# Batches 0 to 10 sorted and worked as a set of their own, in groups of four tiles

## The chip, the core and the metric

The kernel runs on one core of a Trainium2 chip. The metric is the device time of one execution in microseconds (us); lower is better. The engines are TensorE (PE; its weight loads are listed apart as PEld), VectorE (DVE), ScalarE (ACT) and GpSimd (POOL); SP issues DMAs only. The engines run side by side, each through its own list of instructions in order, and wait for one another by semaphores.

## The reference

16 batches of 128 rows of width 128 go through two layers. Layer 0 is attention with 16 heads (queries from x, keys and values from 77 context rows and x) and a feed-forward of butterfly matrices; layer 1 is attention over 77 context rows in which each head keeps its 32 largest scores, and then a feed-forward with 8 experts. Cut to the last part, which the change is about:

```python
x = hidden_states.reshape(-1, h)                    # 16 x 128 rows
route = jax.nn.sigmoid(x @ Wr + br)
max_prob = jnp.max(route, axis=1, keepdims=True)
max_ind = jnp.argmax(route, axis=1)
for e in range(n_experts):                          # 8
    mask = (max_ind == e)[:, None].astype(x.dtype)
    y = jax.nn.gelu(x @ W1[e], approximate=False) @ W2[e]
    out = out + mask * y
out = out * max_prob
```

Each row needs one expert only. W1 is 8 x 128 x 512, W2 is 8 x 512 x 128, all float32.

## The kernel before

**The pipeline of batches.** Everything up to the router's logits is done batch by batch in a pipeline of steps (`run_steps`, `step`). In step i six batches are in work: P = i (inputs), A = i-1 and A2 = i-2 (first attention and its output), B = i-3 (feed-forward 0 and the second attention's scores), C = i-4 (its top 32, on DVE with MAX8 and MATCH_REPLACE8), E = i-5 (output, router). Each step has 8 slots, and the code of each engine lists by hand what it does in which slot; a pair such as (17, 5) below is step 17, slot 5. Steps 16 to 20 have no new batch: A is last present in 16, A2 in 17, B in 18, C in 19, E in 20.

**The sorting.** The experts are worked on sorted rows. For a range of batches (`ROUTES`: 0 to 10, 11 to 14, 15) DVE adds the router's bias (`route_biases`), ACT takes the exponential (`route_exps`), DVE finds each row's expert (`choose`), TensorE counts the rows of each expert by matmuls with ones (`count_rows`), and DVE turns the counts into a place for each row (`row_places`). POOL then scatters each batch's 128 rows to DRAM (`place_row`, one indirect DMA each, line 617). With all 16 batches counted, DVE works out for each of 23 tiles of 128 sorted rows which expert it has and where it begins (`map_tiles`). 23 = 16 + 8 - 1 is the most that 2,048 rows in 8 experts can fill.

**The tiles.** Behind the last batch SP loads the tiles (`load_tile`, line 386, into a ring of 12) and ACT's queue loads their W1 (`load_up`). TensorE turns a tile (line 716), multiplies it by W1 (`tile_up`, line 1161), ACT takes the GELU, TensorE multiplies by W2 (`tile_down`, line 1171), DVE scales and adds the residual (line 1771), and POOL scatters the rows to the output (line 704). Two tiles overlap.

The order of everything is the order in which the code is written, engine by engine; there is no scheduler.

## Time and profile before

| | us |
|---|---|
| median of three runs | 732.41 (731.75 to 734.16) |
| the profiled execution | 734.37 |
| its span in the trace | 732.6 |
| busy in it: PE, DVE, ACT, POOL | 651.1, 571.1, 481.2, 446.9 |

The page divides the span into 40 slices of 18.3 us. TensorE is over 90% busy in slices 5 to 31, until about 577 us, and then at 60 to 70%; its granted clock falls there from full speed to half. DVE stays near 90% until about 640 us. From 680 us TensorE is full again, with the 23 tiles. Of the chain that ended last 49% is TensorE and 35% DVE. Times such as "at 577.09" are us from the start of the span.

### The profile page before, as it was taken

What the parts mean: (1) busy time and instruction counts of PE and PEld (TensorE: products, weight loads), DVE (VectorE), ACT (ScalarE), POOL (GpSimd) and SP (SyncE); (2) the same over time, 40 slices, a digit from 0 to 9 for tenths busy, and PEclk for the clock granted to TensorE, in tenths of its full rate; (3) what the DMA queues carried; (4) which work ended last, traced back from release to release, by engine and by line L of the source; (5) the groups of instructions that cost most, each with busy time, mean ns of one, the idle gap of its engine ahead of it and who ended that gap; (6) DMA issues with size and microseconds to landing.
All of it is one profiled execution on the core that took longest, in us unless ns stands there. A gap on an engine that the chain in (4) does not pass through costs nothing.

```text
span 732.6 us, 19295 instructions
## 1 busy us (share of the span) xinstructions
PE 651.1 (89%) x4994; PEld 529.2 (72%) x4994; DVE 571.1 (78%) x3740; ACT 481.2 (66%) x1331; POOL 446.9 (61%) x689
## 2 busy tenths in 40 slices
PE   5588999999999999999999999999999876772995
PEld 4455677778787787878787878778786764551995
DVE  3255747898989999998989898999999998943231
ACT  1247578888878797888878887878787634221221
POOL 7364667857657575756576765757575536543344
PEclk9779999999999999999999999999999755555998
DMA  7300039992000000000000000000000000003772
GB/s 204 76 1 1 1 105 309 318 294 70 1 3 1 1 1 0 0 0 0 0 0 0 0 0 0 0 0 0 0 1 2 1 0 28 32 23 116 210 205 64
DMA packets 38537, 37.92 MB, mean 52 GB/s; under 512 B 3633, under 2 KB 34249, under 8 KB 38484
## 3 DMA queue, kind: packets, MB, share of 16 engines
q1 hardware_dynamic: 32986, 27.76, 13.6%
q10 hardware_dynamic: 3994, 6.36, 3.1%
q0 software_dynamic: 1504, 3.17, 1.2%
q8 instruction: 24, 0.39, 0.2%
q14 instruction: 29, 0.24, 0.1%
HBM read 16.28 MB, written 21.45 MB: 52 GB/s over the span
## 4 chain that ended last, share of the span: by engine, by line
PE 49%; DVE 35%; issue 6%; POOL 3%; SPq 3%; DMA 2%; ACT 2%; DVEq 0%; POOLq 0%
DVE sw L1564 14%; DVE m L1558 9%; PE bank L716 8%; PE bank L874 6%; PE bank L816 5%; PE bank L945 5%; PE bank L884 4%; PE score_banks L846 3%; DVE negmax L1511 3%; PE bank L1161 3%; PE bank L1171 3%; PE bank L826 2%; PE bank L804 2%; PE bank L908 2%; PE bank L899 2%
## 5 line engine op out<-in xcount | busy, mean ns | idle before, releaser
L1564 DVE MATCH_REPLACE8 sw<-m,sw 128x77 f32<-128x77 f32 x1024 | 219.6, 221 | 0.1
L1558 DVE MAX8 m<-sw 128x8 f32<-128x77 f32 x1024 | 188.8, 225 | 2.3 <-ACT sw L1189 1.3
L1189 ACT ACTIVATE prob<-score_banks,negmax 128x205 f32<-128x205 f32 x256 | 107.2, 431 | 21.3 <-DVE negmax L1511 21.3
L485 POOL TENSOR_TENSOR prob<-prob,inv 128x820 f32<-128x820 f32 x64 | 99.4, 1553 | 18.7 <-DVE inv L1516 18.7
L504 POOL TENSOR_TENSOR sw<-sw,m 128x616 f32<-128x616 f32 x64 | 77.9, 1217 | 50.1 <-DVEq L1545 49.7
L945 PEld LDWEIGHTS bank<-v,p1T 77*128 77x128 f32 x512 | 72.6, 216 | 16.3 <-DVE c_z L1590 6.1
L945 PE MATMUL bank<-v,p1T 77*128 (+1 forms) x512 | 72.5, 269 | 10.9 <-DVE c_z L1590 5.4
L1564 DVE MATCH_VALUE_LOAD sw<-m,sw 128x8 f32 x1024 | 76.6, 75 | 0.0
L1511 DVE TENSOR_REDUCE negmax<-score_banks 128x2 f32<-128x410 f32 x128 | 68.1, 573 | 2.7 <-PE score_banks L846 2.7
L716 PE MATMUL bank<-ident,prob 128*77 128x128 f32 (+1 forms) x512 | 67.3, 275 | 1.6 <-POOL prob L485 1.4
L1189 ACT ACTIVATE h_ring<-bank 128x256 f32<-128x256 f32 (+1 forms) x87 | 38.5, 443 | 45.5 <-PE bank L1161 35.5
L826 PE MATMUL bank<-raw,kvT 128*77 128x512 f32 (+1 forms) x128 | 66.7, 603 | 0.0
L716 PEld LDWEIGHTS bank<-ident,prob 128*77 128x77 f32 (+1 forms) x512 | 58.7, 146 | 9.3 <-POOL prob L485 5.1
L816 PE MATMUL bank<-kvT,raw 128*128 128x205 f32 x256 | 60.4, 359 | 1.2 <-DVE xs L1523 0.6
L928 PE MATMUL bank<-second_keys,b_q 128*128 128x308 f32 x128 | 53.2, 500 | 9.1 <-ACT p1T L1189 8.8
L846 PE MATMUL score_banks<-k_sb,q_sb 64*128 64x205 f32 x512 | 58.7, 348 | 0.0
L511 POOL TENSOR_TENSOR p<-sw 128x308 f32<-128x308 f32 x64 | 46.9, 733 | 18.4 <-ACT sw L1189 18.2
L874 PE MATMUL bank<-ptc,z_ring 77*64 77x128 f32 x512 | 53.7, 287 | 3.3 <-issue 2.6
L816 PEld LDWEIGHTS bank<-kvT,raw 128*128 128x128 f32 x256 | 43.2, 192 | 16.1 <-issue 14.5
L1189 ACT ACT_TABLE_LOAD x34 | 43.6, 1283 | 15.9 <-issue 15.3
L1189 ACT ACTIVATION_READ_ACCUMULATOR prob<-score_banks,negmax 128x1 f32 x256 | 52.9, 207 | 0.0
L874 PE MATMUL bank<-ptl,z_ring 128*64 128x128 f32 x512 | 50.6, 274 | 0.0
(235 smaller groups left out, 1446.7 us busy)
## 6 DMA issues: line engine op xcount, KB each, us to landing
z_sorted<-no_row SPq DMA_DIRECT2D x1, 17415.0 KB, 65.6
raw<-in_L_ffn_W ACTq DMA_DIRECT2D x23, 256.0 KB, 3.4
z_ring<-z_sorted SPq DMA_DIRECT2D x23, 129.0 KB, 3.4
w<-in_L_ffn_W SPq DMA_DIRECT2D x8, 256.0 KB, 4.5
raw<-in_L_xattn_Wkv SPq DMA_DIRECT2D x2, 512.0 KB, 11.2
xs<-in_x SPq DMA_DIRECT2D x1, 960.0 KB, 7.2
cx<-in_ctx SPq DMA_DIRECT2D x1, 577.5 KB
raw<-in_L_xattn_Wq SPq DMA_DIRECT2D x1, 512.0 KB, 10.4
```

The lines of the kernel that those rows point to most:

```text
L485: g.tensor_tensor(p, p, inv[:, 4 * q:4 * q + 4].unsqueeze(2).to_broadcast([128, 4, KV]), ALU.mult).then_inc(s["p_norm"], 1)
L504: g.tensor_tensor(v, v, m8[:, 4 * q:4 * q + 4, 0, 0:1].to_broadcast([128, 4, 2 * NK]), ALU.subtract).then_inc(s["sub_done"], 1)
L716: return nc.tensor.transpose(dst, src, ident[0:rows, 0:rows])
L816: last = mm(dst[:, KV * c:KV * c + KV], wkv_in[:, at:at + 128], kvT[:, :], start=True, stop=True)
L826: mm(dst[0:nr, :], kvT[:, r0:r0 + nr], wkv_in[:, INNER + 512 * j:INNER + 512 * j + 512], start=True, stop=True)\
L846: last = mm(SC[:, u, KV * r:KV * r + KV], q_sb[rows[u], q // 2, 2 * (q % 2) + r, :], k_sb[rows[u], q % 2, r, :], start=False, stop=(r == 1 ...
L874: last = mm(dst[64 * u:64 * u + 64, 128 * c:128 * c + 128], v[:, DH * h:DH * h + DH], p[:, 2 * c + u, :], start=not last_part, stop=last_p ...
L945: last = mm(M[:, c:c + D1 + 1], p1T[:, n, :], v1[:, bass.ds(b, 1), 4 * q + n, :].squeeze(1), start=True, stop=True)
L1189: return nc.scalar.activation(dst, src, f, **kw)
L1511: v.tensor_reduce(negmax[:, 2 * p:2 * p + 2], SC[:, :, KV * (p % 2):KV * (p % 2) + KV], AX_X, ALU.max, negate=True).then_inc(s["max_ready" ...
L1558: v.max(m8[:, h, r, :], sw[:, h, src, :]).then_inc(s[name], 1)
L1564: v.match_replace(sw[:, h, 1, :], m8[:, h, r, :], sw[:, h, src, :], TAKEN)\
```

## The change

The rows of batches 0 to 10 become a set of their own, with its own sorted DRAM tensor, counts and map; batches 11 to 15 are the second set. A set of n batches can fill n + 7 tiles: 18 and 12, together 30 in place of 23.

- The choosing for batches 0 to 10 moves from step 17 to step 16 on DVE and ACT, the counting from (17, 5) to (16, 4) on TensorE, into bank M in place of a score bank (DVE copies the counts out first), the places from (17, 7) to (16, 4), and a first `map_tiles` stands at (16, 5) on DVE.
- POOL's eleven scatters, one in each slot of steps 18 and 19 (11 slots) before, stand in four bunches: 3 at (16, 5), 2 at (16, 6), 3 at (17, 2), 3 at (17, 3).
- The 18 tiles are worked in groups of four: TensorE turns four, then four times W1, then four times W2; ACT copies the turned tiles out, takes four GELUs and scales four results; POOL adds the residual for the group and scatters four times. SP loads tiles and W1 of this set.
- Groups 0 and 1 lie in steps 17 to 20. Groups 2, 3 and 4 (4, 4 and 2 tiles) stand behind step 20, with the counting of batch 15 between the second and third tile of group 2. The 12 tiles of the second set follow in the old manner, two by two. SP loads the first four W1 of the second set, and then its tiles.
- W1's ring becomes 4, the rings of turned tiles and GELUs become 4. Some loads at the start share a semaphore. Nothing changes in steps 0 to 15.

```diff
-    SORTED = NB + NE - 1
-    UPS = 3
+    EARLY = 11
+    SETS = ((0, EARLY), (EARLY, NB))
+    TILES = (EARLY + NE - 1, NB - EARLY + NE - 1)
+    FIRST = (0, TILES[0])
+    GROUP = 4
+    GROUPS = (TILES[0] + GROUP - 1) // GROUP
+    SORTED = sum(TILES)
+    UPS = GROUP
     ROW = 2 * D + 2
     COEF, TOKEN = 2 * D, 2 * D + 1
     NOWHERE = 1 << 20
-    ROUTES = ((0, 11), (11, 15), (15, NB))
+    ROUTES = ((0, EARLY), (EARLY, 15), (15, NB))
...
-        PLACE_AT = {(18 + b // 8, b % 8): (b,) for b in range(ROUTES[0][1])}
+        PLACE_AT = {(16, 5): range(0, 3), (16, 6): range(3, 5), (17, 2): range(5, 8), (17, 3): range(8, EARLY)}
+        DRAIN_GROUPS = 2
+        COUNTS_KEPT = 7
...
             sp.wait_ge(s["map_ready"], 2)
-            sp.wait_ge(s["rows_placed"], 16 * NB)
-            for n in range(SORTED):
+            sp.wait_ge(s["rows_placed"], 16 * EARLY)
+            for n in range(GROUP):
+                load_tile(n)
+            sp.wait_ge(s["o_psum"], NB)
+            for n in range(GROUP):
+                load_early_up(n)
+            for n in range(GROUP, 2 * GROUP):
+                load_tile(n)
+            for n in range(GROUP, FIRST[1]):
+                load_early_up(n)
+                if n + GROUP < FIRST[1]:
+                    load_tile(n + GROUP)
+            sp.wait_ge(s["map_ready"], 4)
+            for n in range(FIRST[1], FIRST[1] + UPS):
+                load_early_up(n)
+            sp.wait_ge(s["late_placed"], 16 * (NB - EARLY))
+            for n in range(FIRST[1], SORTED):
...
+            def store_group(k):
+                u = GROUP * k % RING
+                pool.wait_ge(s["y_scaled"], k + 1)
+                end_u = u + group_size(k)
+                g.tensor_tensor(y_tile[:, u:end_u, :], y_tile[:, u:end_u, :], z_tile[:, u:end_u, D:2 * D],
+                                ALU.add).then_inc(s["y_added"], 1)
+                pool.wait_ge(s["y_added"], k + 1)
+                for n in range(GROUP * k, GROUP * k + group_size(k)):
+                    store_tile(n)
...
+                        if i == 20:
+                            store_group(1)
...
+                        if i == 18:
+                            store_group(0)
...
+            def turn_tiles(k):
+                if k == 0:
+                    reach(pe, "pt_ready", NB - 1, QUADS)
+                else:
+                    pe.wait_ge(s["zT_ready"], k)
+                for j in range(group_size(k)):
+                    n = GROUP * k + j
+                    pe.wait_ge(z_loaded[n % RING], 16 * (n // RING + 1))
+                    last = turn(TC[:, 128 * j:128 * j + 128], z_tile[:, n % RING, 0:D])
+                last.then_inc(s["zT_psum"], 1)
+
+            def tiles_up(k, js):
+                pe.wait_ge(s["zT_ready"], k + 1)
+                if k == 0:
+                    reach(pe, "exp_done", NB - 1, SLOTS)
+                    reach(pe, "z_ready", NB - 1, QUADS)
+                if k == DRAIN_GROUPS:
+                    reach(pe, "x2_ready", NB - 1, 1)
+                for j in js:
+                    n = GROUP * k + j
+                    pe.wait_ge(up_loaded[n % UPS], 16 * (n // UPS + 1))
+                    if k:
+                        pe.wait_ge(s["hT_ready"], n - GROUP + 1)
+                    if k and j == GROUP - 1:
+                        pe.wait_ge(s["y_scaled"], k)
+                    for c in range(HC):
+                        last = mm(up_bank(k, j)[:, 128 * c:128 * c + 128], w1_tile[:, n % UPS, 128 * c:128 * c + 128], z_T[:, j, :],
+                                  start=True, stop=True)
+                    last.then_inc(s["up_psum"], 1)
+
+            def tiles_down(k, js):
+                if k == 0:
+                    pe.wait_ge(s["ld_w2"], 16 * NE)
+                if js[0] == 0:
+                    pe.wait_ge(s["hT_ready"], GROUP * k + group_size(k))
+                    pe.wait_ge(s["y_scaled"], k)
+                for j in js:
+                    n = GROUP * k + j
+                    e = pe.value_load(tile_expert[0:1, n:n + 1], min_val=0, max_val=NE - 1)
+                    for c in range(HC):
+                        last = mm(up_bank(k, 3)[:, 128 * j:128 * j + 128], hT[:, j, c, :], w2[:, bass.ds(e, 1), c, :].squeeze(1),
+                                  start=(c == 0), stop=(c == HC - 1))
+                if js[-1] == group_size(k) - 1:
+                    last.then_inc(s["ey_psum"], 1)
...
-                    if i == 17 and slot == 5:
+                    if i == 16 and slot == 4:
                         count_rows(0)
...
+                        if i == 18:
+                            tiles_up(0, (2,))
+                            tiles_up(0, (3,))
+                            turn_tiles(1)
+                        if i == 19:
+                            tiles_up(1, (3,))
...
+                        if i == 17:
+                            turn_tiles(0)
+                        if i == 18:
+                            tiles_down(0, (2,))
+                            tiles_down(0, (3,))
...
+            tiles_up(2, (0,))
+            tiles_up(2, (1,))
             count_rows(2)
-
-            pe.wait_ge(s["ld_w2"], 16 * NE)
-            pe.wait_ge(s["map_ready"], 2)
...
+            def scaled_tiles(k):
+                act.wait_ge(s["ey_psum"], k + 1)
+                for j in range(group_size(k)):
+                    u = (GROUP * k + j) % RING
+                    last = fn(y_tile[:, u, :], up_bank(k, 3)[:, 128 * j:128 * j + 128], ACT.Copy, scale=z_tile[:, u, COEF:COEF + 1])
+                last.then_inc(s["y_scaled"], 1)
...
-                    if (i, slot) in ((17, 0), (20, 0)):
-                        route_biases(0 if i == 17 else 1)
-                    if (i, slot) in ((17, 1), (20, 2)):
-                        choose(0 if i == 17 else 1)
-                    if (i, slot) in ((17, 7), (20, 5)):
-                        row_places(0 if i == 17 else 1)
+                    if (i, slot) in ((16, 0), (20, 0)):
+                        route_biases(0 if i == 16 else 1)
+                    if (i, slot) in ((16, 1), (20, 2)):
+                        choose(0 if i == 16 else 1)
+                    if (i, slot) == (20, 5):
+                        row_places(1)
+                    if (i, slot) == (16, 5):
+                        map_tiles(0)
```

The order of the instructions at the places that matter most. First DVE in slots 4 and 5 of step 16, before: the statistics of E (`c_st`), the maxima of the scores (`negmax`), the top-32 rounds (`m`, `sw`), and the normalised row `r_z` which TensorE turns for the router.

```order
L1529 BN_STATS c_st<-rows_out 128x6 [waits x3_ready]
L1532 BN_AGGR c_mv<-c_st 128x2 [waits c_stats]
L1516 RECIPROCAL inv<-rowsum 128x4 [waits exp_done]
L1511 TENSOR_REDUCE negmax<-score_banks 128x2 [waits s_psum]
...
L1558 MAX m<-sw 128x8 [waits topk_odd] x2
...
L1536 TENSOR_SCALAR r_z<-rows_out,c_mv,c_rs 128x128 [waits crs_ready,rz_kept]
```

And now, where `counts`, `place` and `tile_expert` are the copied counts, the rows' places and the first result of the map:

```order
L1733 TENSOR_REDUCE negmax<-score_banks 128x2 [waits s_psum]
...
L1862 COPY counts<-bank 128x136 [waits count_psum,c_past]
L1865 TENSOR_TENSOR place_e<-counts,expert_base 128x88 [waits r_step]
L1866 TENSOR_TENSOR place_e<-place_e,chosen 128x88 [waits r_step]
L1867 TENSOR_REDUCE place_f<-place_e 128x11 [waits r_step]
L1868 CAST place<-place_f 128x11 [waits r_step]
...
L1878 TENSOR_TENSOR n_full<-counts,steps 128x8x11
...
L1892 TENSOR_SCALAR tile_expert<-t_exp 128x18
L1758 TENSOR_SCALAR r_z<-rows_out,c_mv,c_rs 128x128 [waits crs_ready,rz_kept]
```

Five instructions for the places (the copy is new, the others stood in step 17) and eleven for the map (which stood behind the last batch alone) are now between the maxima and `r_z`.

TensorE in slots 5 to 7 of step 17, before: a quarter of the second attention's scores (`second_keys,b_q`), the counting, the turn of `r_z`, the last quarter, the feed-forward 0 of batch 15 (`f_zT,w_up`) and the logits (`wr,r_zT`).

```order
L1011 MATMUL score_banks<-chosen,before_p 128x88 [waits chosen_ready,exp_done,c_past]
...
L928 MATMUL bank<-second_keys,b_q 128x308 [waits kbd_ready,q_ready,p1T_ready]
L716 MATMUL bank<-ident,r_z 128x128 [waits rz_ready,fT_ready]
L928 MATMUL bank<-second_keys,b_q 128x308 [waits kbd_ready,q_ready,sc_ready]
L945 MATMUL bank<-v,p1T 128x9 [waits p1T_ready,rT_ready]
...
L899 MATMUL bank<-f_zT,w_up 128x128 [waits fT_ready,sc_ready]
...
L972 MATMUL bank<-wr,r_zT 128x8 [waits rT_ready]
```

And now:

```order
L991 MATMUL bank<-second_keys,b_q 128x308 [waits kbd_ready,q_ready,p1T_ready]
L778 MATMUL bank<-ident,z_ring 128x128 [waits z_loaded0,pt_ready]
L778 MATMUL bank<-ident,z_ring 128x128 [waits z_loaded1]
L778 MATMUL bank<-ident,z_ring 128x128 [waits z_loaded2]
L778 MATMUL bank<-ident,z_ring 128x128 [waits z_loaded3]
L778 MATMUL bank<-ident,r_z 128x128 [waits rz_ready,fT_ready]
L991 MATMUL bank<-second_keys,b_q 128x308 [waits kbd_ready,q_ready,sc_ready]
...
L1117 MATMUL bank<-z_T,raw 128x128 [waits z_ready,up_loaded0,exp_done,zT_ready]
...
L962 MATMUL bank<-f_zT,w_up 128x128 [waits fT_ready,sc_ready]
L1035 MATMUL bank<-wr,r_zT 128x8 [waits rT_ready]
L1117 MATMUL bank<-z_T,raw 128x128 [waits z_ready,up_loaded1,exp_done,zT_ready]
```

The counting has gone from here, and the turns of the first four tiles, which wait for their loads, stand ahead of the last quarter of the scores; two tiles' W1 matmuls stand around the feed-forward.

## Rows read from the trace of the kernel before

**Rows 1.** Busy us by stretch: PE, PEld, DVE, ACT, POOL (instructions); PEclk, DMA, GB/s
```profile
543.00:577.00 34.00, 32.50 (x270) 26.29 (x269) 32.28 (x219) 27.31 (x76) 21.64 (x39) 1.00 0.01 2
577.00:612.00 35.00, 26.17 (x125) 22.18 (x125) 31.92 (x220) 14.35 (x30) 12.77 (x19) 0.61 0.00 1
612.00:646.00 34.00, 23.48 (x80) 17.46 (x80) 31.71 (x251) 9.46 (x20) 23.23 (x28) 0.50 0.11 39
646.00:663.00 17.00, 10.87 (x56) 9.18 (x56) 5.24 (x23) 3.09 (x9) 5.29 (x10) 0.50 0.03 9
663.00:677.00 14.00, 2.00 (x36) 1.68 (x37) 5.11 (x26) 1.49 (x2) 3.99 (x5) 0.50 0.47 146
677.00:724.00 47.00, 45.10 (x381) 44.33 (x380) 13.76 (x43) 13.73 (x23) 20.08 (x21) 0.96 0.67 188
```

**Rows 2.** Timeline of DVE, starts of steps 17 and 18: start, us, line, operation, out<-in
```profile
577.09 0.28 DVE L1529 BATCH_NORM_STATS2 b_st<-xs 128x6 f32<-128x128 f32 x1
...
611.99 0.29 DVE L1529 BATCH_NORM_STATS2 b_st<-xs 128x6 f32<-128x128 f32 x1
```

**Rows 3.** Timeline of DVE, choosing and placing the rows of batches 0 to 10
```profile
576.18 0.99 DVE L1608 TENSOR_TENSOR route<-route,br 128x88 f32<-128x88 f32 x1
...
579.48 0.44 DVE L1618 TENSOR_SCALAR route<-route 128x88 f32<-128x88 f32 x1
...
582.12 0.34 DVE L1536 TENSOR_SCALAR b_z<-xs,b_mv,b_rs 128x128 f32<-128x128 f32 x1
...
604.33 0.24 DVE L1639 TENSOR_TENSOR place_e<-score_banks,expert_base 128x88 f32<-128x88 f32 x1
...
605.17 1.84 DVE L1642 CAST place<-place_f 128x11 uint32<-128x11 f32 x1
```

**Rows 4.** Timeline of DVE, the last placing and the map of the tiles
```profile
666.70 0.15 DVE L1642 CAST place<-place_f 128x1 uint32<-128x1 f32 x1
666.77 0.28 DVE L1648 TENSOR_TENSOR n_full<-score_banks,steps 128x128 f32<-128x128 f32 x1
...
669.49 0.17 DVE L1662 TENSOR_SCALAR tile_expert<-t_exp 128x23 int32<-128x23 f32 x1
```

**Rows 5.** Timeline of TensorE at its two clocks, and in step 17
```profile
548.37 1.95 PE L884 MATMUL bank<-raw,h_ring 128*128 128x128 f32 x16
...
582.85 3.64 PE L884 MATMUL bank<-raw,h_ring 128*128 128x128 f32 x16
...
597.62 1.40 PE L928 MATMUL bank<-second_keys,b_q 128*128 128x308 f32 x2 [0.22 <-ACT p1T L1189]
...
606.50 1.91 PE L908 MATMUL bank<-wd,f_h 128*128 128x128 f32 x8
```

**Rows 6.** Timeline of POOL in step 17 and step 20
```profile
588.11 0.55 POOL L493 TENSOR_TENSOR f_rs<-f_rs,half 128x1 f32<-128x1 f32 x1
...
589.18 1.22 POOL L504 TENSOR_TENSOR sw<-sw,m 128x616 f32<-128x616 f32 x1 [0.52 <-DVEq L1545]
...
659.85 0.19 POOL L491 TENSOR_SCALAR c_rs<-c_mv 128x1 f32<-128x1 f32 x1 [9.60 <-DVE c_mv L1532]
```

**Rows 7.** Chain of waits from the last scatters to the first loads
```profile
665.99 0.96 POOL z_sorted L617
...
667.25 2.80 DMA z_sorted<-rows_out,place
...
672.22 4.18 DMA z_ring<-z_sorted
```

**Rows 8.** Chain of waits, two tiles in the middle of the tail
```profile
690.05 0.90 PE bank L1161 x8
...
691.95 0.89 PE bank L1161 x8
```

**Rows 9.** Timeline of ACT, a change of table in step 17
```profile
607.36 1.28 ACT L1189 ACT_TABLE_LOAD   x1
608.65 0.72 ACT L1189 ACTIVATE sw<-sw 128x616 f32<-128x616 f32 x1
```

More of the change, by code:

```diff
@@ L698, in _ @@
             place_row(NB - 1)
[L699 to L706 removed]
+            store_group(2)
+            store_group(3)
+            store_group(4)
+            for n in range(FIRST[1], SORTED):
+                pool.wait_ge(s["ey_ready"], n - FIRST[1] + 1)
+                store_tile(n)
             for u in range(RING):
@@ L1010, in count_rows @@
                 pe.wait_ge(s["chosen_ready"], n + 1)
-                last = mm(S0[:, b0 * NE:b1 * NE], before_p[:, :], rows[:, b0 * NE:b1 * NE], start=True, stop=b1 == 1,
+                last = mm(dst[:, b0 * NE:b1 * NE], before_p[:, :], rows[:, b0 * NE:b1 * NE], start=True, stop=b1 - c0 == 1,
                           skip_group_check=True)
-                for k in range(1, b1):
-                    b = max(b0, k)
-                    last = mm(S0[:, b * NE:b1 * NE], ones_bf[:, :], rows[:, (b - k) * NE:(b1 - k) * NE], start=False,
-                              stop=(k == b1 - 1), skip_group_check=True)
@@ L1017, in count_rows @@
-                if b1 == NB:
-                    for b in range(NB):
-                        last = mm(S1[:, 0:NE], ones_bf[:, :], chosen[:, b, :], start=(b == 0), stop=(b == NB - 1))
-                last.then_inc(s["count_psum"], 1)
+                for k in range(1, b1 - c0):
+                    b = max(b0, c0 + k)
+                    last = mm(dst[:, b * NE:b1 * NE], ones_bf[:, :], rows[:, (b - k) * NE:(b1 - k) * NE], start=False,
+                              stop=(k == b1 - c0 - 1), skip_group_check=True)
@@ new lines, in count_rows @@
+                if b1 == SETS[k0][1]:
+                    for b in range(c0, b1):
+                        last = mm(dst[:, (NB + k0) * NE:(NB + k0 + 1) * NE], ones_bf[:, :], chosen[:, b, :], start=(b == c0),
+                                  stop=(b == b1 - 1), skip_group_check=True)
+                last.then_inc(s["count_psum"], 1)
+            def turn_tiles(k):
[8 more added lines that the diff above has]
+                last.then_inc(s["zT_psum"], 1)
@@ L1173, in tile_down @@
                 last.then_inc(s["ey_psum"], 1)
-            turn_z(0)
-            turn_z(1)
-            tile_up(0)
-            for n in range(SORTED):
+            turn_z(T0)
+            turn_z(T0 + 1)
+            tile_up(T0)
+            for n in range(T0, SORTED):
                 if n + 1 < SORTED:
@@ L1289, in route_exps, with turned_tiles, tile_gelus @@
                 fn(route[:, b0:b1, :], route[:, b0:b1, :], ACT.Exp, scale=-1.0).then_inc(s["r_exp"], 1)
+            def turned_tiles(k):
+                act.wait_ge(s["zT_psum"], k + 1)
+                if k:
+                    act.wait_ge(s["up_psum"], GROUP * k)
+                n = 128 * group_size(k)
+                copy(z_T[:, :, :].rearrange("p u q -> p (u q)")[:, 0:n], TC[:, 0:n]).then_inc(s["zT_ready"], 1)
+            def tile_gelus(k, js):
+                if k:
+                    act.wait_ge(s["ey_psum"], k)
+                for j in js:
+                    act.wait_ge(s["up_psum"], GROUP * k + j + 1)
+                    fn(hT[:, j, :, :].rearrange("p c q -> p (c q)"), up_bank(k, j)[:, :], ACT.Gelu).then_inc(s["hT_ready"], 1)
+            def scaled_tiles(k):
[4 more added lines that the diff above has]
+                last.then_inc(s["y_scaled"], 1)
             def step(i, at):
@@ L1402, in _ @@
             route_exps(2)
+            tile_gelus(2, (0,))
+            tile_gelus(2, (1,))
+            tile_gelus(2, (2,))
+            tile_gelus(2, (3,))
+            turned_tiles(3)
+            scaled_tiles(2)
+            tile_gelus(3, (0,))
+            tile_gelus(3, (1,))
+            tile_gelus(3, (2,))
+            tile_gelus(3, (3,))
+            turned_tiles(4)
+            scaled_tiles(3)
+            tile_gelus(4, (0,))
+            tile_gelus(4, (1,))
+            scaled_tiles(4)
             def load_up(n):
@@ L1637, in row_places @@
                 dve.wait_ge(s["count_psum"], n + 1)
-                places = S0[:, b0 * NE:b1 * NE].rearrange("p (b e) -> p b e", b=nb)
-                then(v.tensor_tensor(pe_, places, expert_base[:, :].unsqueeze(1).to_broadcast(wide), ALU.add))
+                if n == 0:
+                    then(v.tensor_copy(counts[:, :], M[:, 0:(NB + 1) * NE]))
+                src = counts if n == 0 else S0
+                places = src[:, b0 * NE:b1 * NE].rearrange("p (b e) -> p b e", b=nb)
+                then(v.tensor_tensor(pe_, places, base.unsqueeze(1).to_broadcast(wide), ALU.add))
                 then(v.tensor_tensor(pe_, pe_, ch, ALU.mult))
```

255 lines of the change are left out of this document (171 added, 84 removed).

## The prediction

> **What bounds the kernel now.** I read the slices of the page first, which show where TensorE's share and clock change, and then asked for the busy time of the stretches between these points [rows 1]. In step 16 (543 to 577) the clock is full (1.00, 2.4 GHz), TensorE is busy 32.5 of 34 us and DVE 32.3: both bind, and each has under 2 us to spare. In 577 to 646 (steps 17, 18 and most of 19) DVE is busy 63.6 of 69 us with the top-32 rounds and TensorE 49.7, at a mean clock of 0.61 and 0.50 (0.5 is 1.2 GHz). In 646 to 663 no engine is full: one batch is left, a chain of short pieces. In 663 to 677 TensorE works 2.0 of 14 us: choosing, scatters, map, first loads. From 677 to 724 come the 23 tiles, TensorE 45.1 of 47 us.
>
> So the tail behind 663 is where the change gives, and steps 16 to 20 are where it takes. Steps 0 to 15 stay as they are.
>
> **What the tail gives.** Before, 61 us lie between 663 and TensorE's end at 724. After, 10 early tiles and 12 late ones lie there, with no idle stretch ahead of them. I walk it with these prices: a tile costs 1.90 in steady work (690.05 to 691.95, [rows 8]), 0.9 of it for each of its two multiplications and 0.1 for the turn between; at 1.2 GHz a part is 1.7, by the ratio of 3.64 to 1.95 for one block of 16 matmuls at the two clocks [rows 5].
> - Group 2: the clock is low when it starts, since TensorE was busy 10.9 of the 17 us before [rows 1], and rises after some full work, as it did here from 0.50 in 663 to 677 to a mean of 0.96 in 677 to 724. Two W1 parts at 1.7, the counting 0.9, two at 0.9, turns 1.1, four W2 parts 3.6: 10.8, to 673.8.
> - Group 3: 3.6 + turns 0.5 + a wait for the last GELU 0.5 + 3.6 = 8.2, to 682.0. Group 4: two W1 parts 1.8, to 683.8; wait 1.0, two W2 parts 1.8, to 686.6.
> - The late tiles start late. On SP their first load stands behind the loads of W1 for tiles 18 to 21, and the last of these waits until tile 17's W1 part is done, at 683.8. One issue takes 1.1 (670.05 to 672.22 for two), and a tile then lands in about 3 to 4.2 (4.18 for the second) [rows 7]. Tile 18 is issued at 686.0, is there at 689.2, tile 19 at 690.3: TensorE waits 3 us or so that are in no list of instructions.
> - Twelve tiles from 690.5: 12 x 1.90 + 0.9 for the first W1 part = 23.7, to 714.2.
>
> The last store behind that costs the same as before. The tail ends 9.8 us sooner; I take **10**. With the clock at 2.4 GHz from the start it is 11.4, with 3 us more of waiting for loads or stores 7. So the 14 idle us before the tiles are nearly all won, and 7 additional tiles (13.3 us) are paid, less the 8 tiles (15.2 us) that have moved into steps 17 to 20.
>
> **What the steps pay.** Step 16 is the stretch to 577 [rows 1]; step 17, between the two starts on DVE, lasts 34.9 us [rows 2].
>
> Step 16. DVE gets the choosing for 11 batches: 582.12 - 579.48 = 2.6 us [rows 3], 0.4 for waiting on ACT's exponential, 0.3 for the bias; the places: three operations of 0.28 each (604.33 to 605.17), a copy of some 0.3, and the cast; the map: 666.77 to 669.66 is 2.9 for 23 tiles and 16 batches [rows 4], I take 2.7 for the smaller set. The cast took 1.84 for these 11 batches and 0.15 for one [rows 3, 4]; I take 1.0. Sum 8.1. Of this at most 1.7 fits in DVE's idle time [rows 1]. TensorE gets 22 short matmuls (some 1.2 us), and it stops three times: for `b_z` behind the choosing, for the copied counts ahead of the turn into M, for `r_z` behind places and map. After idle time of that kind at 577 its clock fell and the same 16 matmuls took 3.64 instead of 1.95 [rows 5]; in step 16, where it also binds, I charge 1.5 for that. 8.1 - 1.1 + 1.5 = **+8.5**; ends 6 (cast 0.15, all slack used, clock stays) and 12 (cast 1.84, no slack, 3 us of clock).
>
> Step 17 loses the bias (0.9, [rows 3]), the places (2.7, 604.33 to 607.0) and the choosing. The last was half hidden: the next thing DVE waits for is TensorE's output projection (582.85 to 586.5, [rows 5]), which starts only when `b_z` is there. It comes 1.4 earlier with the choosing gone, not 2.6, as POOL's two scatters of (16, 6) delay the root that `b_z` needs. Together **-5.0**.
>
> Then the wait. TensorE's turn of tiles 0 to 3 at (17, 5) waits for their loads, and these for the last of the eleven scatters. With S the start of step 17 (577.09 before): POOL's root for A2 ended at S + 11.5 (588.11 + 0.55, [rows 6]) and ends at about S + 9.4 now. Behind it stand six scatters at 1.26 each (665.99 to 667.25, [rows 7]) and one subtraction of 1.22 [rows 6]: the last starts at S + 17.0 and lands 2.8 later [rows 7]. SP issues four loads at 1.1: S + 24.2, and the fourth is there some 3 us later (between the 2.8 of a scatter and the 4.18 of a load that had company, [rows 7]): S + 27.2. TensorE stands at the turn from S + 20.5 (599.0 before, less 1.4). Behind the wait, in its order, are what took 9.4 us before (599.0 to 608.4, [rows 5]) up to the feed-forward's output that closes step 17 on DVE, and two new W1 parts: 13 us at 1.2 GHz; as it is all dense work the clock should rise in it, and I take 10.6, so S + 37.9. DVE would be ready at S + 29.9. So step 17 lasts 37.9, **+3.0** against 34.9 (8.0 of waiting less 5.0). Ends: -5 (the rows come in time) and +6 (clock low throughout, 40.3, and the scatters later).
>
> Step 18. Ahead of `b_z`'s turn, which starts the chain to batch 15's first scores, stand two W1 parts and four turns (2.9 at 2.4 GHz, 5.2 at 1.2), and ACT has to change its table to GELU and back, 1.28 each [rows 9]. Against it the chain runs faster if the clock is up. **+1.3**, between 0 and 5. The scatters of step 18 are gone from POOL, and the group's add and four scatters come in their place.
>
> Four changes of table are added in all, 5.1 us on an engine that is busy 24 of 69 us [rows 1]. The Trainium skill (ScalarE: Activation LUTs, "What ACT_TABLE_LOAD costs") counts 1283 ns for the load and 1380 ns of drain for each. Here the next activation starts 0.01 us after the load [rows 9], so the trace shows the first part only; by the rule steps 18 and 19 would each be up to 1.4 longer on ACT's chain.
>
> Steps 19 and 20. Four W1 parts, four turns and four W2 parts (8.3 at 2.4 GHz) stand among the last batch's pieces; TensorE's idle time in 646 to 663 is 6.1 [rows 1], most of it in waits that they don't fill. The denser work should raise the clock, worth some 1.5 on the pieces of that chain. On POOL group 1's add and four scatters (about 6.2) stand at (20, 3) ahead of the root of the last batch, and start when ACT has scaled the group, about 656.5 in the old times; the root, at 659.85 before [rows 6], waits until 662.6. 2.7 - 1.5 = **+1.2**; ends -3 and +6.
>
> **The sum.** 8.5 + 3.0 + 1.3 + 1.2 = 14.0 paid, 10 given: +4.0. Span 732.6 -> 736.6, the profiled execution 734.37 -> 738.4. That execution is 2.0 above the median of the runs shown (732.41), so the median should be **736.4**. What a measurement of this kernel tells from no change is about 0.3%, 2.2 us: 730.2 to 734.6 is "the same".
>
> **The rivals.**
> - *The holes take it.* DVE's idle 5.4 us and TensorE's 19.3 in 577 to 646 [rows 1] hold the eight tiles, and the rows are there when (17, 5) comes: 7.5 - 5.0 + 1.0 - 0.5 = 3.0 paid, 11 given, -8: 724.4. For it: total TensorE idle time is above the 15.2 us of eight tiles, and I have charged each wait in full, where one may cover another. Against it: scatters, issue and landing add up to 18 us behind POOL's root, and step 17 has 11 for them.
> - *Half the wait.* The wait in step 17 costs DVE 4 rather than 8: 10.0 paid, 10 given: 732.4, the same.
> - *TensorE at 1.2 GHz becomes the bound of the drain.* It has 49.7 us of work in 69 at about that clock; eight tiles at 3.6 add 29. Then from (17, 5) TensorE sets the pace and not DVE: 10 + 5 + 4 + 4 = 23 paid, 9 given, +14: 746.4. It decides if the clock does not rise above 0.6 in steps 17 to 19. Against it: it rose whenever TensorE had been full for a while, as in the tail.
> - *It doesn't do what it says*: the order shows the groups where they are meant to be; if all tiles were late, the spans of the groups would show behind the last logits. I give it no chance of its own.
>
> **How the numbers follow.** The forecast 0.47, with its own range 733 to 742; the holes 0.26; half the wait 0.15; the low clock 0.12. Faster: the first rival and a little of the second, 0.31. The same: the rest of the second and the lower edge of the forecast, 0.14. Slower: 0.55. The range 724 to 748 leaves out the better end of the first rival and the worse of the third.
>
> **What would show it.** Right: DVE's step 16 (between its `b_st` starts) 42 us or so; TensorE idle 5 to 8 us ahead of the first `ident,z_ring` matmul, with the DMA as its releaser; DVE waiting for `xs` behind it; POOL's last root late behind `out_x`; a hole of about 3 us ahead of tile 18. Wrong: step 17 under 32 us with no wait at the turn (first rival), or TensorE over 95% busy at 0.5 from step 17 on (third).

## The result and the profile after

The changed kernel takes 745.26 us (median of 4, 744.13 to 746.69) against 732.79 before (median of 4, 731.75 to 734.16): a ratio of 1.0172, 95% interval 1.0151 to 1.0192, so 12.5 us slower. The forecast was 736.4. The sign was right, the size was not: 4.0 more were forecast, 12.5 came.

The page's slices (busy tenths) show that TensorE's idle time moved and did not go. Before, TensorE worked 2 of the 14 us ahead of the tiles [rows 1], the slice at 2 tenths in this line of the kernel before:

```profile
PE   5588999999999999999999999999999876772995
```

In the changed kernel (TensorE, VectorE, and the clock) no slice is that empty, but all of the last ten are at 4 to 8 tenths:

```profile
PE   6588999999999999999999999999997747875885
DVE  3365639899999989898999999898989794944021
PEclk9889999999999999999999999999999957887998
```

The same in stretches: busy us of PE, PEld, DVE, ACT and POOL (with instructions), the clock, the share of DMA and GB/s. The rows are step 16, step 17, step 18 (to VectorE's `c_z` of batch 14), steps 19 and 20 (to the last `route<-route,br`), and the tail:

```profile
539.60:582.00 42.40, 36.00 (x289) 28.95 (x289) 37.73 (x242) 27.91 (x79) 23.45 (x42) 0.92 0.05 18
582.00:620.20 38.20, 24.32 (x132) 19.88 (x131) 26.55 (x206) 12.63 (x27) 22.62 (x27) 0.69 0.27 84
620.20:651.50 31.30, 21.97 (x145) 18.38 (x144) 24.96 (x202) 14.40 (x30) 13.01 (x17) 0.89 0.22 61
651.50:680.00 28.50, 17.60 (x109) 15.87 (x110) 11.73 (x72) 11.73 (x25) 13.76 (x20) 0.75 0.17 50
680.00:742.40 62.40, 46.81 (x380) 43.77 (x379) 11.85 (x48) 17.87 (x37) 28.54 (x30) 0.94 0.44 129
```

The kernel before, profiled once more and cut at the same events (`b0` below):

```profile
540.30:574.30 34.00, 32.42 (x269) 26.20 (x269) 32.33 (x219) 27.28 (x76) 21.65 (x36) 1.00 0.01 2
574.30:609.20 34.90, 27.16 (x125) 23.02 (x125) 31.83 (x219) 14.37 (x30) 12.70 (x18) 0.56 0.00 1
609.20:637.20 28.00, 19.50 (x65) 14.23 (x65) 25.88 (x203) 8.00 (x17) 17.92 (x23) 0.50 0.11 38
637.20:660.20 23.00, 14.82 (x71) 12.41 (x71) 11.09 (x72) 4.57 (x12) 10.62 (x16) 0.50 0.05 18
660.20:730.80 70.60, 48.42 (x423) 47.26 (x423) 19.53 (x70) 15.23 (x25) 26.64 (x28) 0.84 0.54 154
```

| us | before (both profiles) | after | change | forecast |
|---|---|---|---|---|
| step 16 | 34.0, 34.1 | 42.5 | +8.4 | +8.5 |
| step 17 | 34.9, 34.9 | 38.2 | +3.3 | +3.0 |
| step 18 | 28.0, 28.0 | 31.3 | +3.3 | +1.3 |
| steps 19, 20 | 23.0, 23.0 | 28.5 | +5.5 | +1.2 |
| tail | 69.6, 70.6 | 62.4 | -7.2 to -8.2 | -10 |
| sum | 189.6, 190.5 | 202.8 | +12.3 to +13.3 | +4.0 |

The sum agrees with the medians (12.5). The two spans, 732.6 and 742.4, differ by only 9.8, because step 16 began at 543.05 in the profile of before and at 539.57 in that of after. From here on I compare from the start of step 16.

Step 16 on VectorE (start, us, line, operation, idle before it): the bookkeeping now stands between two batches' work, and the next start, `b_st`, is at 582.03:

```profile
561.20 1.48 DVE L1866 TENSOR_TENSOR place_e<-place_e,chosen 128x88 f32<-128x88 f32 x1
...
562.99 0.17 DVE L1868 CAST place<-place_f 128x11 uint32<-128x11 f32 x1
...
568.32 0.17 DVE L1892 TENSOR_SCALAR tile_expert<-t_exp 128x18 int32<-128x18 f32 x1
...
582.03 0.29 DVE L1751 BATCH_NORM_STATS2 b_st<-xs 128x6 f32<-128x128 f32 x1
```

Step 17 on TensorE, the turn of tiles 0 to 3. In brackets is the idle time and its releaser; the four waits are 5.9 us:

```profile
606.51 0.45 PE L778 MATMUL bank<-ident,z_ring 128*128 128x128 f32 x1 [3.99 <-DMA z_ring<-z_sorted]
607.64 0.47 PE L778 MATMUL bank<-ident,z_ring 128*128 128x128 f32 x1 [0.69 <-DMA z_ring<-z_sorted]
608.81 0.48 PE L778 MATMUL bank<-ident,z_ring 128*128 128x128 f32 x1 [0.69 <-DMA z_ring<-z_sorted]
609.80 0.47 PE L778 MATMUL bank<-ident,z_ring 128*128 128x128 f32 x1 [0.51 <-DMA z_ring<-z_sorted]
```

VectorE stands idle behind it for 6.32 us, until the feed-forward's output of batch 15:

```profile
619.75 0.35 DVE L1745 SCALAR_TENSOR_TENSOR xs<-bank,tg,xs 128x128 f32<-128x128 f32 x1 [6.32 <-PE bank L971]
```

GpSimd in steps 18 to 20. Twice, an add and four scatters stand as one block of 7 us ahead of what a batch waits for, the subtraction of its top-32 chain at 649.96 and the last root at 676.87:

```profile
643.03 1.18 POOL L674 TENSOR_TENSOR raw<-raw,z_ring 128x512 f32<-128x512 f32 x1 [2.67 <-ACT raw L1356]
645.04 1.07 POOL L666 DMA_INDIRECT out_x<-raw,z_ring  x1 [0.83 <-POOL raw L674]
...
648.98 0.97 POOL L666 DMA_INDIRECT out_x<-raw,z_ring  x1 [0.30 <-issue]
649.96 1.24 POOL L544 TENSOR_TENSOR sw<-sw,m 128x616 f32<-128x616 f32 x1
...
669.93 1.18 POOL L674 TENSOR_TENSOR raw<-raw,z_ring 128x512 f32<-128x512 f32 x1 [5.92 <-ACT raw L1356]
...
675.83 0.97 POOL L666 DMA_INDIRECT out_x<-raw,z_ring  x1 [0.30 <-issue]
676.87 0.19 POOL L531 TENSOR_SCALAR c_rs<-c_mv 128x1 f32<-128x1 f32 x1
```

TensorE behind these two blocks (652 and 678), and in the tail: it waits at the first W2 part of each group, and for the first late tiles:

```profile
652.03 1.11 PE L778 MATMUL bank<-ident,p 128*77 128x128 f32 x4 [3.39 <-POOL p L551]
...
686.86 1.15 PE L1131 MATMUL bank<-w,h_ring 128*128 x8 [1.17 <-ACT h_ring L1356]
...
696.97 4.75 PE L1131 MATMUL bank<-w,h_ring 128*128 x32 [1.27 <-issue]
...
705.00 2.29 PE L1131 MATMUL bank<-w,h_ring 128*128 x16 [1.49 <-ACT h_ring L1356]
708.02 0.30 PE L778 MATMUL bank<-ident,z_ring 128*128 128x128 f32 x1 [0.73 <-DMA z_ring<-z_sorted]
...
715.91 1.16 PE L1328 MATMUL bank<-z_T,raw 128*128 128x128 f32 x8 [1.34 <-DVE z_T L2000]
```

On VectorE the last batch's r_z has the second block in front of it:

```profile
677.83 0.35 DVE L1758 TENSOR_SCALAR r_z<-rows_out,c_mv,c_rs 128x128 f32<-128x128 f32 x1 [3.29 <-POOL c_rs L533]
```

### The profile page after: what moved, and what is told of

Read it like the earlier page. It is cut to its first block and busy times, and to the rows that moved or that the text cites. A ratio compares the mean times of both kernels' runs of the same rounds, so it can differ in the third digit from the quotient of the medians.

```text
span 742.4 us, 19674 instructions
## 1 busy us (share of the span) xinstructions
PE 654.4 (88%) x5091; PEld 532.5 (72%) x5091; DVE 563.6 (76%) x3730; ACT 496.4 (67%) x1365; POOL 458.8 (62%) x704
## 5 line engine op out<-in xcount | busy, mean ns | idle before, releaser
L1008 PEld LDWEIGHTS bank<-v,p1T 77*128 77x128 f32 x512 | 64.2, 195 | 8.1 <-issue 3.5
L1008 PE MATMUL bank<-v,p1T 77*128 (+1 forms) x512 | 64.1, 252 | 4.3 <-ACT r_zT L1356 1.5
L551 POOL TENSOR_TENSOR p<-sw 128x308 f32<-128x308 f32 x64 | 46.8, 731 | 29.8 <-ACT sw L1356 29.7
L991 PE MATMUL bank<-second_keys,b_q 128*128 128x308 f32 x128 | 50.5, 477 | 9.7 <-ACT p1T L1356 9.7
L1356 ACT ACTIVATE sw<-sw 128x616 f32<-128x616 f32 x64 | 46.8, 732 | 11.7 <-POOL sw L544 11.5
```

What stands on the lines that cost most here:

```text
L1008: last = mm(M[:, c:c + D1 + 1], p1T[:, n, :], v1[:, bass.ds(b, 1), 4 * q + n, :].squeeze(1), start=True, stop=True)
L1356: return nc.scalar.activation(dst, src, f, **kw)
```

## The experiments

The theory after the result: the changed kernel loses on waits that can be taken away one by one (z loads in step 17, GpSimd's two store blocks, the first W2 part of each tail group), beside VectorE's work in step 16. The rival: engines are full in the drain, a wait taken away comes back as another. One table ahead, in us (the kernels' ratios are with their texts). The stretches come from one profiled execution of each kernel, the median from all its executions:

| kernel | 16 | 17 | 18 | 19, 20 | tail | from 16 | median |
|---|---|---|---|---|---|---|---|
| after | 42.5 | 38.2 | 31.3 | 28.5 | 62.4 | 202.8 | 745.26 |
| e1 both stores late | 42.8 | 38.5 | 29.9 | 20.4 | 68.6 | 200.2 | 746.21 |
| e2 turn late | 43.1 | 30.8 | 31.5 | 29.4 | 62.4 | 197.1 | 741.0 |
| e6 GELUs behind | 42.7 | 38.4 | 29.8 | 30.2 | 62.3 | 203.5 | 747.28 |
| e3 all groups behind | 43.1 | 30.6 | 27.1 | 23.9 | 85.8 | 210.6 | 755.35 |
| e7 e2 and map later | 39.9 | 32.4 | 34.1 | 29.5 | 63.2 | 199.2 | 742.06 |
| e8 e2 and tail | 43.0 | 31.5 | 34.9 | 28.5 | 58.1 | 196.0 | 741.75 |
| e9 e1 and SP's order | 43.2 | 38.1 | 30.1 | 22.6 | 62.9 | 196.8 | 740.21 |
| e10 group 1's store late | 42.5 | 38.5 | 29.9 | 26.2 | 62.6 | 199.7 | 743.14 |
| c1 combined | 43.3 | 30.9 | 34.0 | 20.4 | 62.4 | 191.0 | 735.48 |
| c2 c1 and map later | 39.9 | 32.5 | 33.2 | 20.4 | 62.5 | 188.5 | 733.33 |
| c3 c1 and GELUs behind | 42.8 | 32.2 | 35.4 | 23.0 | 62.5 | 195.9 | 736.97 |

The kernel before ran beside them with medians of 734.38 (e1, e2, e6, e3), 733.55 (b0, e7 to e9) and 733.54 (c1 to c3, e10).

**b0, the kernel before again.** No edit.

> The kernel before, unchanged, profiled once more. What is open is the 3.5 us by which the changed kernel's first 16 steps were shorter in its one profile (step 16 starts at 539.57 against 543.05; at 541.5 to 542.2 in four variants of it). Theory A (execution to execution variation and no effect of the change): step 16 starts here anywhere from 540 to 543, within the range of the variants. Theory B (the change shortens the start by 1 to 3 us): it starts at 542.5 or later again.

Step 16 starts at 540.26, against 543.05 in the first profile of the same kernel. The changed kernel and its variants lie between 539.6 and 543.0. The 3.5 us at the start are variation between executions, theory A. Steps 16 to 20 agree within 0.1 us between the two profiles; the tails differ by 1.0.

**e2, the turn later.**

```
 step 17, slot 5: - turn_tiles(0)        slots 6, 7: - tiles_up(0, (0,)), tiles_up(0, (1,))
 step 17, slot 7: + turn_tiles(0)        step 18, slot 0: + tiles_up(0, (0,)), tiles_up(0, (1,))
 ACT:  turned_tiles(0) from step 17, slot 5, to slot 7
```

> The changed kernel with the first group's turn moved from the middle of step 17 (before scores of pair 3) to its end, and its first two up products into step 18. Theory A (TensorE's 5.9 us of waits for z loads in step 17 are on the path): step 17 shortens from 38.2 to 33 to 35 us and the whole falls by 3 to 5 us, to 740 to 742 us. Rival B (step 17 is set by the batch's own chain over VectorE and GpSimd, and the wait only stood in its shadow): step 17 stays within 1 us of 38.2, the whole within 1 us of 745.3. Rival C: the up products meet ScalarE's GELUs later and step 18 grows by what step 17 loses, the whole again near 745.

Ratio to before 1.0093 (1.0075 to 1.0111) instead of 1.0172. Step 17 takes 30.8 us instead of 38.2, a larger fall than theory A gave it, and step 18 takes 31.5 with two W1 parts more. From step 16 on 5.7 us are won. At the turn's new place one short wait is left of the four:

```profile
611.67 0.48 PE L778 MATMUL bank<-ident,z_ring 128*128 128x128 f32 x1 [0.52 <-DMA z_ring<-z_sorted]
```

The forecast's step for the wait (8.0) was right in kind and size: 7.4 us come back when the turn moves. Of the runs with this move step 18 is shortest here. Its first two W1 parts ran at the full granted clock (1.00):

```profile
615.22 2.03 PE L1117 MATMUL bank<-z_T,raw 128*128 128x128 f32 x16
```

In the five later runs with the same move (e7, e8, c1, c2, c3) the same 16 matmuls ran at 0.50 to 0.51, took 3.66 to 3.76 us, and step 18 took 33.2 to 35.4.

**e3, no tile inside the steps.** The groups' calls in steps 17 to 20 are moved behind the last step, but for the turn of group 0, which goes to step 19; `DRAIN_GROUPS = 0`.

> The changed kernel with no tile work inside steps 17 to 20 (only the turn of group 0 is in step 19): sorting of batches 0 to 10 stays in steps 16 and 17, all five groups run behind the last batch. Theory A (tiles inside the steps cost less than behind them, but much more than forecast): steps 17 to 20 fall back by about 12 us (5 in step 17, 3.3 in 18, 5.5 in 19 and 20), the tail grows by two groups at the 9.8 us of group 3, 19.6; the whole is about 752 us. Rival B (tiles inside cost as much as behind): the whole is within 2 us of 745.3 or lower. Step 16 stays at 42 us under both; if it falls back to 34, tile work has to do with it.

Ratio 1.0295 (1.0275 to 1.0315). This run separates the two halves of the change. Sorting early without tiles costs 9.1 in step 16, gives 4.3 in step 17 (5.0 were forecast) and 0.9 in step 18, and takes 0.9 in 19 and 20. The tiles inside the steps cost 7.6 us in step 17 and 8.8 in 18 to 20 (59.8 against 51.0), 16.4 in all, and 23.4 behind them, 11.7 a group. Tiles inside are cheaper, but by 7.0 and not by the 23.4 that they would save if they were hidden. Stretches of step 18 to the tail:

```profile
615.90:643.10 27.20, 18.46 (x65) 13.34 (x65) 24.79 (x203) 8.22 (x18) 10.02 (x15) 0.54 0.10 29
643.10:667.00 23.90, 15.53 (x66) 13.27 (x67) 11.09 (x73) 5.17 (x13) 7.26 (x13) 0.50 0.00 1
667.00:752.80 85.80, 66.82 (x516) 62.29 (x515) 11.89 (x48) 25.88 (x54) 38.64 (x40) 0.92 0.48 135
```

**e1, both stores later.**

```
 POOL, step 18, slot 6: - store_group(0)      step 19, slot 7: + store_group(0)
 POOL, step 20, slot 3: - store_group(1)      behind place_row(NB - 1): + store_group(1)
```

> The changed kernel with its two in-step stores moved on GpSimd: group 0's sum and four scatters behind step 19's last add_rows instead of inside step 18's masking chain, group 1's behind the scatter of batch 15 instead of ahead of batch 15's last root. Theory A (GpSimd's bursts stand on the path twice): TensorE's waits of 3.39 us ahead of `ident,p` at 652 and 5.28 us ahead of r_z at 678 shrink to under 1 and about 2 us; the whole falls by 4 to 7 us, to 738 to 741 us. Rival B (another chain, ScalarE's or VectorE's, ends at the same points): the waits stay with another releaser and the whole is within 1.5 us of 745.3. Rival C (the stores now come too late for the ring of 12): a new wait ahead of the turns of groups 3 or 4, the whole above 747 us.

Ratio 1.0169 (1.0151 to 1.0187): nothing on the whole. Rival C comes nearest, but not as written: the median is under 747, and the new wait is not for a z load. Steps 19 and 20 fell by 8.1 us, as theory A has it, and the tail grew by 6.2. On SP's queue the W1 loads stand behind z loads that wait for these stores, and TensorE waits for a W1 load with no releaser in the list (SP's issues first, then TensorE):

```profile
684.62 0.34 SPq L404 DMA_DIRECT2D z_ring<-z_sorted  x1
685.74 0.34 SPq L410 DMA_DIRECT2D raw<-in_L_ffn_W  x1
```

```profile
688.56 1.76 PE L1116 MATMUL bank<-z_T,raw 128*128 128x128 f32 x7 [2.02 <-issue]
```

**e9, e1 with SP's queue in another order.** Behind z load 11: W1 loads of tiles 8 to 11, z loads 12 to 15, W1 loads 12 to 15, z loads 16 and 17, W1 loads 16 and 17.

```
-            for n in range(GROUP, FIRST[1]):
+            for n in range(GROUP, 2 * GROUP):
                 load_early_up(n)
-                if n + GROUP < FIRST[1]:
-                    load_tile(n + GROUP)
+                load_tile(n + GROUP)
+            for k in (2, 3):
+                for n in range(GROUP * k, GROUP * k + GROUP):
+                    load_early_up(n)
+                for n in range(GROUP * k + GROUP, GROUP * k + GROUP + group_size(k + 1)):
+                    load_tile(n)
+            for n in range(4 * GROUP, FIRST[1]):
+                load_early_up(n)
```

> The kernel with the late stores, with SP's queue in another order: W1 loads of tiles 8 to 15 ahead of the z loads that wait for those stores. The late stores shortened steps 18 to 20 by 9.5 us, and the tail grew by 6.2. Theory A (W1 loads of tiles 13 and on stood behind z loads that waited for stores of group 1): the tail returns to 63 to 65 us, the whole to 740 to 742. Rival B (the tail is set by something fixed to the last batch's chain or to the z loads of tiles 16 and 17 themselves): the tail stays over 67 us and the whole at 745 or above.

Ratio 1.0084 (1.0055 to 1.0112). The tail returned to 62.9, theory A, and 5.9 of the 8.1 us won in steps 19 and 20 stayed:

```profile
653.80:676.30 22.50, 15.63 (x106) 13.75 (x105) 11.13 (x72) 8.62 (x21) 12.32 (x18) 0.77 0.24 67
```

The wait of 3.39 us for `p` is gone, and the one for the last r_z has shrunk from 5.28 to 2.56; what is left is the batch's own chain:

```profile
674.61 0.45 PE L783 MATMUL bank<-ident,r_z 128*128 128x128 f32 x1 [2.56 <-DVE r_z L1763]
```

**e10, only group 1's store later**, with e9's order on SP.

> The changed kernel with only group 1's store moved behind the scatter of batch 15 and SP's W1 loads ahead of z loads, group 0's store still in step 18. It splits the 7 us of both stores (step 18 1.1, steps 19 and 20 5.9 with both moved). Theory A: the step-20 burst alone stands for 3.3 us (VectorE's wait of 3.29 us ahead of r_z), group 0's for the rest: steps 19 and 20 take 25 to 26 us, step 18 stays at 31.3, the whole is about 742. Rival B (group 0's burst is the whole loss, since batch 15 then comes late to the root anyway): steps 19 and 20 stay at 28 to 28.5. Rival C (group 1's is the whole): 22.5 to 23.5.

Ratio 1.0129 (1.0089 to 1.0169). Steps 18 to 20 together take 59.8 us in the changed kernel, 56.1 here and 52.7 in e9: group 1's store costs 3.7 and group 0's 3.4. That is nearest to theory A, which had 31.3 for step 18 and 25 to 26 for 19 and 20; 29.9 and 26.2 came. The ratios give the same halves (1.0172, 1.0129, 1.0084: 3.2 and 3.3 us), but the interval of e10 overlaps both others, so the cost of both together is shown, and its split rests on single profiles. In e1, both stores late without SP's new order, the three steps took 50.3 us; counted from there group 0's store costs 5.8. I take the three steps together, since the cut between 18 and 19 moved: with the same code step 18 took 29.9 here and 31.3 in the changed kernel. In the changed kernel VectorE stood idle for 1.42 us ahead of the operation that feeds `c_z`, here for 0.53 (first row the changed kernel, second e10), and TensorE's wait for `p` behind group 0's store came 31.7 us after the start of step 18 in both:

```profile
651.22 0.26 DVE L1810 RECIPROCAL c_inv<-bank 128x16 f32<-128x16 f32 x1 [1.42 <-DVE sw L1786]
```

```profile
652.15 0.26 DVE L1815 RECIPROCAL c_inv<-bank 128x16 f32<-128x16 f32 x1 [0.53 <-DVE sw L1791]
...
654.22 1.11 PE L783 MATMUL bank<-ident,p 128*77 128x128 f32 x4 [3.38 <-POOL p L557]
```

**e6, GELUs behind b_q.** ACT, step 18: `tile_gelus(0, ...)` and `turned_tiles(1)` from ahead of `move(B, b_zT, ...)` to behind `second_probs_out(C, 1)`.

> The changed kernel with ScalarE's four GELUs of group 0 and the copy of group 1's turned tiles moved in step 18 from ahead of b_zT to behind the copy of p1T that follows b_q. Theory A (GELUs and two table loads ahead of b_zT delay the last batch's queries): TensorE's waits of 1.84 us (b_zT) and 1.77 us (p1T) go, step 18 falls from 31.3 to 28 to 29.5 us, the whole to 742 to 744 us. Rival B (the down products are then late, or a later ScalarE step is): the waits move to the first down product or to c_zT, the whole is within 1 us of 745.3 or above.

Ratio 1.0178 (1.0149 to 1.0208), rival B. Step 18 is 29.8, as in e10 without the edit, and 19 and 20 grew by 1.7. This change of ScalarE's order wins nothing.

**e7, the map later**, on top of e2: `map_tiles(0)` from step 16, slot 5, to step 17, slot 2.

> The kernel of the late turn (group 0's turn at the end of step 17) with VectorE's ten steps that map tiles to experts moved from step 16, slot 5, to step 17, slot 2. Theory A (VectorE sets step 16, so everything put there is paid in full, while step 17 waits elsewhere): step 16 falls by 3 to 4 us, from 43.1 to about 39.5, step 17 grows by 0 to 2; the whole falls by 2 to 4 us against the kernel of the late turn (741.0), to 737 to 739. Rival B (the same work is paid wherever it stands): step 17 grows by as much, the whole within 1 us of 741.

Ratio 1.0122 (1.0072 to 1.0172); e2's 1.0093 lies within this interval. The steps moved as theory A has it and the whole as rival B: step 16 fell by 3.2 and step 17 took 1.7 of it. That VectorE's work is paid in full in step 16 holds. Step 18 took 2.6 more than in e2, with its first two W1 parts at the lower clock, so the whole didn't gain.

**e8, the tail**, on top of e2: down products of groups 2 to 4 in banks X, M and S1, each behind its own tile's GELU; z loads 18 to 21 ahead of their W1 loads.

```
+            return S0 if k < DRAIN_GROUPS else {2: X, 3: M, 4: S1}[k]
...
+                    if k >= DRAIN_GROUPS:
+                        pe.wait_ge(s["hT_ready"], n + 1)
```

> The kernel of the late turn with a changed tail alone: down products of groups 2, 3 and 4 go to banks of their own, each waits for its own tile's GELU and not for the whole group's; SP issues the z loads of tiles 18 to 21 ahead of their W1 loads. Theory A (the tail loses 1.2 to 1.5 us at each of three groups to that wait and 2.5 us at the first late tiles to the queue): the tail falls from 62.4 to 57 to 59 us, the whole to 736 to 738. Rival B (DMA traffic of W1 loads sets the pace there, shown as waits without a releaser): the tail falls by under 1.5 us, the whole is 739.5 or above.

The tail fell by 4.3, theory A's size, but the whole did not move against e2: ratio 1.0109 (1.0081 to 1.0136). Step 18, whose code is e2's, took 34.9 instead of 31.5 in the profiled run: there the first two W1 parts ran at the lower clock (0.50), 3.76 us where e2 had 2.03:

```profile
616.80 3.76 PE L1123 MATMUL bank<-z_T,raw 128*128 128x128 f32 x16
```

The tail's gain is seen in one profile and not in the medians.

**c1, c2, c3, the edits together.** c1 is e2, e9 and e8; c2 adds e7's edit, c3 e6's.

> The changed kernel with three edits together: the late turn of group 0, the late stores with SP's W1 loads ahead of the z loads that wait for them, and the tail with banks of its own for the down products and z loads first. Counted from the start of step 16 to the end (the execution's length before that varies by 3 us) the changed kernel took 202.8 us, the late turn alone gave 5.7, the late stores with SP's new order 6.0, the tail 4.3. Theory A (three separate waits, savings add): 186.8 us, the whole 727 to 731 us, faster than the kernel before (733.5, 189.5 to 190.5 from step 16). Rival B (the savings overlap: the late stores crowd the tail that the tail edit shortens, or TensorE at its lower clock eats a part): 190 to 193 us, the whole 731.5 to 735. If it is above 735 the theory of separate waits falls.

> The combined kernel with VectorE's mapping of tiles moved from step 16 to step 17, slot 2. In the pair tried before, step 16 gave back 3.2 us, step 17 took 1.7 and step 18 2.6 (in an execution in which TensorE's clock was low under its up products). Theory A (step 18's 2.6 were a matter of the clock and not of the move): 1 to 2 us less than the combined kernel. Rival B (the W1 and z loads that need the map come later): equal to the combined kernel or up to 2 us more.

> The combined kernel with ScalarE's GELUs of group 0 behind the batch's b_q and p1T in step 18. With the stores still in the way it shortened step 18 by 1.4 us and lengthened steps 19 and 20 by 1.7. Theory A (the loss behind it came from GpSimd's store that waited for ScalarE's later scaling, and is gone with the late stores): 1 to 2 us less than the combined kernel. Rival B (ScalarE's chain is only reordered): within 1 us of it or above.

Ratios to before: c1 1.0021 (0.9997 to 1.0046), c2 1.0003 (0.9982 to 1.0023), c3 1.0034 (1.0009 to 1.006). For c1 rival B was right: 191.0 us from step 16 instead of 186.8, with a median just above the 735 at which the expectation gave up separate waits. Steps 17, 19 and 20 keep their gains; of e8's tail nothing is left (62.4), and step 18 stays at 34:

```profile
617.20:651.20 34.00, 27.78 (x175) 24.36 (x176) 24.96 (x202) 17.11 (x34) 9.91 (x15) 0.82 0.29 80
651.20:671.60 20.40, 13.07 (x97) 11.18 (x96) 11.20 (x73) 8.41 (x20) 12.41 (x18) 0.88 0.22 63
```

For c2 theory A has the sign (2.1 us by the medians), but the intervals overlap. c3 gained nothing. So the changed kernel can be brought level with the kernel before, and no run is shown to be faster than it.

## Why the prediction was wrong in size

- **Step 16, +8.5: right** (+8.4; 9.1 by e3). The total was partly luck. The cast, charged at 1.0 us, took 0.17, and the multiply took 1.48 instead of some 0.28 (see the end). Against the kernel before VectorE was busy 5.4 us more in this step and idle 3.0 more (37.73 of 42.40 against 32.33 of 34.00), where the prediction has 7.7 of added work, 0.4 of waiting for ScalarE, 1.1 of idle time filled and 1.5 for the clock. e7 shows that what leaves VectorE there comes back in full.
- **Step 17, +3.0: right** (+3.3), part by part: -4.3 for the removed work against -5.0, +7.6 for the wait against +8.0 (e3), 7.4 back in e2. TensorE waited 5.9 us at the turn and VectorE 6.3 behind it.
- **Steps 18 to 20: the step that failed**, +2.5 forecast (1.3 and 1.2), +8.8 measured. In its working of steps 19 and 20 the prediction had "on POOL group 1's add and four scatters" ahead of the root of the last batch, at 2.7 us; the block cost 3.7 (e10). In the changed kernel's own trace the root starts 2.9 us later behind `c_mv` than in e9, near the 2.7, so this term was small by 1 at most. The same block of group 0, ahead of a subtraction that ScalarE and then TensorE wait for, was named under step 18 ("the group's add and four scatters come in their place") and priced at nothing; it cost 3.4 (e9 less e10). What is left, 1.7 us in e9 against 51.0 in both profiles of before, is all that eight tiles' W1 and W2 parts, ScalarE's GELUs and its table loads cost here, where the forecast has -0.2. So the two blocks on GpSimd are 7.1 of the 8.8, and 4.4 of the 6.3 that were missed; counted from e1 (50.3) they are 9.5, and nothing is left. These are single profiles, and the gap between e1 and e9 is of the size of what is left. The 1.5 credited to a faster clock can't be seen in the changed kernel's length, although the clock rose (0.50 to 0.89 and 0.75). With the blocks out of the way the length fits it: in e1, c1 and c2 steps 19 and 20 take 20.4 us with the tiles' parts in them, 2.6 less than before, at a clock of 0.88 (c1).
- **The tail, -10: too much by 2 to 3.** From the start of group 2's first W1 part to tile 18's I had 27.5 us and 29.5 came: group 2 12.1 instead of 10.8, group 3 9.8 instead of 8.2, group 4 5.7 instead of 4.6, the hole ahead of tile 18 about 2 instead of 3.9. The waits for a GELU were reckoned at nothing, 0.5 and 1.0 for the three groups and took 1.2, 1.3 and 1.5. One more of 1.34 came among the late tiles, which were reckoned at an unbroken 1.90.
- **The rivals.** The first fell: there was no slack that hid the tiles. The second fell: the wait of step 17 cost 7.4 to 7.6 and not 4. The third gave nearly the right time (746.4) by another way: TensorE was neither the bound nor held at 0.5 (clock 0.69 to 0.89 in steps 17 and 18, busy 64 and 70% there).

What stays open: why step 18 takes 33 to 35 us in e7, e8, c1, c2 and c3 and 31.5 in e2. The low clock on the first two W1 parts is 1.6 to 1.7 us of it in each of them; why the clock had risen in e2 by then and not in the others, and what the rest is, was not separated. Open too is what VectorE waited for ahead of `c_inv` in the changed kernel. That wait ends with GpSimd's subtraction (649.96 to 651.20), but in e1 the same operation of VectorE began inside that subtraction, so this is no more than a neighbour.

## What to carry to other kernels

When work is moved into a pipeline's drain, follow each engine that it issues on to the next instruction which another engine waits for, and charge the whole block there: here GpSimd's add with four scatters, 7 us, stood twice on such a place and cost some 3.4 and 3.7, and only one was charged. A wait for data can be passed by moving its consumer two slots: here that gave back 7.4 us in step 17, though what was moved then met the lower clock in five of six profiles, and step 18 grew. Moving a producer later needs a look at every in-order queue that its result releases: in e1 SP's queue took back 6.2 of the 9.5 us won in steps 18 to 20, until its loads were reordered.
